# Two graph layers on one core: the edge features of a chunk loaded in two transfers of four tiles in place of one of eight

## The reference, cut

```python
def layer0(x, edge_attr_3, W, root, gamma, beta, src, dst):
    # B: [E, 8] products of the three attributes or their complements
    z = (B[:, :, None] * x[src][:, None, :]).reshape(E, 8 * 64)
    agg = segment_sum(z @ W.reshape(8 * 64, 64), dst)
    out = agg / max(cnt, 1)[:, None] + x @ root
    return elu(batchnorm(out, gamma, beta))

def layer1(x, edge_attr_64, W1, b1, W2, b2, gamma, beta, src, dst):
    agg = segment_sum(x[src] + edge_attr_64, dst)
    return batchnorm(relu(agg @ W1 + b1) @ W2 + b2, gamma, beta)

x = layernorm(x + layer0(x, ...))
x = layernorm(x + layer1(x, ...))
```

## Time and profile before

| | |
|---|---|
| median of 3 runs | 760.03 us |
| lowest, highest | 753.52, 762.93 us |
| profiled execution: span from first to last instruction | 739.4 us |
| profiled execution: whole time | not given; the median less the span is 20.6 us |
| TensorE, weight loads, VectorE busy | 575.8, 434.3, 448.4 us |
| ScalarE, GpSimd busy | 377.2, 382.3 us |
| DMA traffic | 48.70 MB, 89134 packets |

### The profile page before, as it was taken

The page is one execution under the profiler, slowest core; times in us unless marked ns, Lnnn a source line. Parts: engine busy times, 40 slices in busy tenths (PEclk is TensorE's granted clock), DMA queues, the critical chain, the costliest instruction groups (busy, mean ns, idle before and its releaser), DMA issues.

```text
span 739.4 us, 16650 instructions
## 1 busy us (share of the span) xinstructions
PE 575.8 (78%) x4151; PEld 434.3 (59%) x4152; DVE 448.4 (61%) x1622; ACT 377.2 (51%) x663; POOL 382.3 (52%) x382
## 2 busy tenths in 40 slices
PE   4455889688777878787877878877887679869994
PEld 2334667566665656676665656756666567734542
DVE  7934657455464646465564556645664567587975
ACT  8344656365555655565565566565632233343044
POOL 6873666466565656565566565666666662000000
PEclk9965888788997978899898989799997868779998
DMA  6421333233242323233233342442412150000002
GB/s 130 109 62 30 94 85 73 59 92 86 68 95 56 97 59 95 68 82 95 60 95 81 71 96 59 94 95 60 97 36 55 37 103 12 3 0 1 1 1 43
DMA packets 89134, 48.70 MB, mean 66 GB/s; under 512 B 76252, under 2 KB 77667, under 8 KB 89069
## 3 DMA queue, kind: packets, MB, share of 16 engines
q1 hardware_dynamic: 75949, 35.40, 19.8%
q0 software_dynamic: 11968, 12.28, 8.6%
q10 hardware_dynamic: 1152, 0.16, 0.2%
HBM read 46.86 MB, written 0.93 MB: 65 GB/s over the span
## 4 chain that ended last, share of the span: by engine, by line
PE 62%; issue 14%; DVE 9%; another core or an unknown queue 5%; DVEq 4%; ACT 2%; ACTq 0%
PE ps L678 14%; PE ps L601 13%; PE ps L638 13%; PE ps L623 5%; PE ps L861 5%; DVEq L1308 3%; PE ps L607 2%; PE ps L866 2%; PE ps L617 2%; DVE pair L1298 2%; DVE agg L1313 1%; PE ps L591 1%; PE ps L712 1%; PE ps L628 1%
## 5 line engine op out<-in xcount | busy, mean ns | idle before, releaser
L528 POOL DMA_INDIRECT rows<-in_x,idx x374 | 381.0, 1019 | 236.0 <-issue 94.1
L601 PE MATMUL ps<-pair,ohp 128*125 128x500 bf16 x416 | 186.0, 450 | 39.2 <-issue 14.4
L1002 ACT CAST adj<-ps 125x500 f32 x208 | 123.8, 595 | 180.6 <-remote 99.2
L678 PE MATMUL ps<-whot,rows 128*128 128x108 f32 x816 | 194.5, 323 | 17.1 <-issue 16.9
L638 PE MATMUL ps<-xs,u 125*128 125x192 bf16 x1050 | 155.3, 274 | 54.3 <-issue 46.2
L678 PEld LDWEIGHTS ps<-whot,rows 128*128 128x128 f32 x816 | 157.9, 229 | 34.9 <-issue 28.5
L1313 DVE TENSOR_TENSOR agg<-agg,ps 128x24 f32 x416 | 75.8, 182 | 151.8 <-remote 74.2
L989 ACT ACTIVATE u<-u,own 128x768 uint8<-128x768 uint8 (+1 forms) x168 | 152.7, 961 | 26.3 <-DMA u<-codes_scratch 25.9
L1298 DVE TENSOR_SCALAR pair<-iota_h,comb 128x500 bf16<-128x500 int16 x416 | 123.6, 358 | 61.8 <-remote 25.6
L638 PEld LDWEIGHTS ps<-xs,u 125*128 125x128 fp8e4 x1050 | 103.0, 111 | 96.2 <-issue 78.9
L1302 DVE TENSOR_SCALAR ohp<-iota_h,srcp 128x125 bf16<-128x125 int16 x416 | 109.8, 275 | 6.3 <-issue 5.1
(11 more groups left out here) (211 smaller groups left out, 383.4 us busy)
## 6 DMA issues: line engine op xcount, KB each, us to landing
u<-codes_scratch SPq DMA_DIRECT2D x42, 400.0 KB
rows<-in_edge_attr SPq DMA_DIRECT2D x51, 256.0 KB
rows<-in_x,idx POOLq DMA_INDIRECT x374
x_now<-in_x SPq DMA_DIRECT2D x25, 31.2 KB
adj<-in_x SPq DMA_DIRECT2D x1, 700.0 KB
xs<-in_x SPq DMA_DIRECT2D x1, 700.0 KB
out<-u SPq DMA_DIRECT2D x3, 224.0 KB
adj<-in_edge_attr SPq DMA_DIRECT2D x1, 576.0 KB
```

The source lines that it names most:

```text
L528: pool.indirect_dma_start(rows[:, s, t, 0:C], None, x, bass.IndirectOffsetOnAxis(ap=idx[:, at:at + 1], axis=0)).then_inc(gathered[0][0] if ...
L601: return nc.tensor.matmul(m_ps[0:PN, bank_of(phase, g), 0:PAIRS], ohp[:, par, t, :], pair[:, par, t, :], start=(n == 0), stop=(n == GROUP ...
L678: last = nc.tensor.matmul(z_ps[:, half, at:at + ZW], rows[:, s, t, :], whot[:, par, t, :], start=True, stop=True)
L1002: nc.scalar.copy(bass.AP(adj, offset=start, ap=[[NT * NA, PN], [NA, NT], [1, GWIN]]), m_ps[0:PN, bank_of(phase, g), 0:PAIRS].rearrange("p ...
```

## The change

Each load of the edge features becomes two, of tiles 0 to 3 and 4 to 7. The first waits for `z_done` of the first half of the slot's chunk, the second for that of the second half. Both count up the same semaphore, which so reaches 32 for a chunk, and TensorE waits for both at the chunk's first product. The last load (L479) becomes one of four tiles and one of three.

```diff
-            def load_ea(c, s):
-                sp.wait_ge(z_done, c * 2 + 2)
-                sp.dma_start(rows[:, s, :, C:P], ea64_full[:, bass.ds(c * CH, CH), :]).then_inc(ea_loaded[s], 16)
+            def load_ea(c, s, half):
+                sp.wait_ge(z_done, c * 2 + (half + 1))
+                at = half * (CH // 2)
+                sp.dma_start(rows[:, s, at:at + CH // 2, C:P], ea64_full[:, bass.ds(c * CH + at, CH // 2), :]
+                             ).then_inc(ea_loaded[s], 16)
...
             for s in range(SLOTS):
-                load_ea(s, s)
+                for half in range(2):
+                    load_ea(s, s, half)
...
             def load_chunk(i, s, taken_too=True):
                 c = i * SLOTS + s
-                load_ea(c, s)
+                for half in range(2):
+                    load_ea(c, s, half)
                 if s % STEP == 0:
                     load_x(i * (SLOTS // STEP) + (s // STEP - 1))
...
-            sp.dma_start(rows[:, SLOTS - 1, 0:CH - 1, C:P], ea64_full[:, FULL - CH + 1:FULL, :]).then_inc(
-                ea_loaded[SLOTS - 1], 16)
+            for half in range(2):
+                at, n = half * (CH // 2), CH // 2 - half
+                sp.dma_start(rows[:, SLOTS - 1, at:at + n, C:P],
+                             ea64_full[:, FULL - CH + 1 + at:FULL - CH + 1 + at + n, :]).then_inc(ea_loaded[SLOTS - 1], 16)
...
                     if t == 0:
-                        pe.wait_ge(ea_loaded[s], i * 16 + 16)
+                        pe.wait_ge(ea_loaded[s], i * 32 + 32)
...
-                pe.wait_ge(ea_loaded[s], i * 16 + 16)
+                pe.wait_ge(ea_loaded[s], i * 32 + 32)
```

## The result

The changed kernel takes 760.63 us (median of 20 runs, 754.79 to 766.0) against 761.75 us for the kernel before (20 runs, 753.52 to 770.64). The ratio of record is 1.0099, 95% interval [1.0064, 1.0135]: 1% slower, and no change at 2%. The two medians, 760.63 / 761.75 = 0.9985, say otherwise, and so do the means, 760.94 / 761.54 = 0.9992 with a half width of 0.0030 (from the scatter of both sets). The ratio of record leaves out runs that lie more than 1.5% above the fastest of their kernel, but that alone doesn't make the 1% here: it takes 3 of the 20 runs of the kernel before (765.1, 765.51 and 770.64 us), the mean of the other 17 is 760.56 us, and 760.94 / 760.56 = 1.0005. The reference that 1.0099 stands for, 760.94 / 1.0099 = 753.5 us, is as low as the lowest of the 20 runs. What the 1% is worth is thus the first question of the experiments.

A forecast was written before the change was run, and what follows sets the result against it. A chunk was taken as a ring of TensorE, VectorE and ScalarE with the codes beside it, the edge features off it. Terms summed to 0: 739.4 + 20.6 + 0 = 760 us, range 750 to 771.

The forecast's parts named there:

- the time around the span: Outside the profiled 739.4 us span: 20.6 us, taken from the 760.03 us median of three runs.
- (d): Start: four issues become eight, done by 24.2 us, under the codes issue at 24.58; term 0 to 0.1 us.
- (f): DMA engines: edge features issued behind the codes on SP's queue don't slow them; term 0, range -4 to +3 us.
- (a): First half's start: in 41 of 51 loads about 0.65 us behind the codes; nobody waits for it, term 0.
- (b): Second half's start: up to 0.65 us later, against 35 us of cover before TensorE needs it; term 0.
- The 27 us: Within (b): upper bound if the cover were gone, 41 x 0.65 us.
- (c): SyncE's own time: 52 more issues, 34 us, spread over a queue that stands waiting; term 0.
- The rival of 794 us: SyncE's queue: each of 52 further issues holds up the codes by 0.65 us, 34 us more; chance 1%.
- the 104 us: Added transfers: about 2 us fixed cost each, 52 x 2 us more if each were waited for.
- (e): End: last loads' halves start earlier; one more issue of 0.4 us lies in both covers; term 0.
- The slower rival (775 us): DMA engines: first half delays the codes by up to 0.67 us in 22 chunks, 15 us more; chance 6%.

The follow-up runs named there:

- three sets: Unedited changed kernel against the kernel before: the result 0.9992 and two repeats, 1.0012 and 1.0005 in the means; weighted together 1.0003 +- 0.0019.
- four transfers: Changed kernel with each chunk's load in four transfers of two tiles, against the kernel before: 759.13 against 758.31 us, means 1.0011, R 1.0040.
- with no cover: Edge loads issued three chunks later, just ahead of use, in the kernel before (whole) and changed one (split): 820.48 and 821.15 us, against 744.90 before.
- with the edge features away: Kernel before with its whole edge transfer issued half a chunk later, against the kernel before: 759.03 against 758.31 us, means 1.0010, R 0.9996.

## Why the prediction was right or wrong

**The forecast**, 760 us and no change, agrees with the two medians (760.63, 761.75) and with the pooled 1.0003 +- 0.0019. It doesn't agree with the ratio of record, whose interval leaves out 1: 1.0099 is some 7.5 us, where my sum had 0 and at most +3 us. If that ratio is right, the step that failed is that every term was put at 0, and which term holds the 7.5 us stays open. The runs don't show it in any: the means of three sets give 1.0003, four transfers cost no more than two, and the landing of the codes is 3.99 us as before. The kernel against itself gave 1.0037, so part of such a ratio is no kernel's; the rest of 1.0099 is unexplained. What the runs do show as wrong in the prediction are a step beside the terms (the time around the span), the size of (d) and the reading in (f).

**The sum around the span failed.** 739.4 + 20.6 was made from the span of one execution and a median that lies 2.5% from its time. What lies around the span is 2 us. That the number came out is no merit of the sum: I had taken the median as the anchor and then found the 20.6 us as the difference. A sum from durations alone would have given 741 us, which lies among the times of two of the chips and 2.5% under the result. The range, from the scatter of three runs, held for this set and the first chip of the experiments; on the other two the changed kernel or its relatives took 742 to 746 us in the mean.

**(a), when the first half starts:** right. 0.64 and 0.66 us behind the codes in the rows above, median 0.77. The change doesn't do what it says, as forecast, and the first half set ahead of the codes shows that doing it would have given nothing.

**(b), the second half:** right in the term, and the cover was more than enough: of the three chunks one is enough, and with none 76 us are lost. The 27 us that I allowed if the cover were gone were far too many: with no cover a split costs 0.7 us in the means (4 runs each), within their scatter (817.98 to 822.87 and 818.29 to 826.52). The step that failed there is that an issue moved by 0.65 us moves the landing by as much.

**(c), SyncE's time:** right; with four transfers it isn't felt either. The rival of 794 us is out, and so is the 104 us estimated from a fixed cost: with every transfer waited for, splitting them costs 0.7 us.

**(d), the start:** the term was right at the end of the account, its size was not. I bounded eight issues by 2 x 2.95 us, 0.74 us each, and held 24.2 us against 24.58; they took 8.50 us, 1.06 each, and the codes went at 27.98. One execution was too little for such a bound: four whole transfers took 2.95 to 4.23 us in five executions, eight halves 4.79 to 8.50 us in five. The cover that I named, the wait for `codes_stored`, was used up; another one that I hadn't named, VectorE's `xs` at 65 us, took it. That the term came out at 0 was luck in the argument, though not a narrow one: in four transfers a delay of 13.2 us was made good too.

**(e), the end:** right, 0.95 us for two issues, and the counts at 619.74, ahead of the last products at 656.0.

**(f), the DMA engines:** the step failed, the term held. "What is issued behind the codes on SP's queue doesn't slow them" was read from two landings; with the edge features away the median falls by 0.39 us. That these two landings agree with ring order wasn't enough: packets of the later transfer begin before the last of the earlier one has ended. This isn't a time in the span: ScalarE's wait for the codes is 25.9, 20.5 and 14.6 us in three kernels, and 18.0 us in the kernel before once more, with no trace of it in the run times. The slower rival (775 us) was right that the edge features delay the codes, and wrong in the size and the path. In the changed kernel the codes land after 3.99 us (median of 16), as before.

**The chances.** Same at 2% was 91%, and it was the case.

## What to carry to other kernels

A transfer that no engine waits for can be split, moved by half a chunk or by two chunks, and the time stays; look first for its name among the waits. An earlier wait condition does nothing where the queue that would see it stands at another wait in front. Before a term is set against one trace, ask from which chip the trace is: here the same kernel differs by 2% between chips and by as much between runs, so that a ratio of 1.01 was no finding until the kernel had been run against itself and the change repeated.

## What the runs showed of the hardware

- The same program took 758.3 us on one chip and 744.7 and 744.9 us on two others (means of 35, 35 and 23 runs). The granted clock was 0.837 in the mean of these runs on the first and 0.849 and 0.848 on the others. Within one chip, runs with 0.01 less of it took 2.5 to 3.0 us more (a line through its runs), so the clock makes an estimated 3 of the 13.5 us; the rest is open.
- What an issue from SyncE takes at the start varies between executions more than with the size of the transfer: four whole ones took 2.95 to 4.23 us (five executions, 0.74 to 1.06 us each), eight halves 4.79 to 8.50 us (five, 0.60 to 1.06), sixteen quarters 17.04 us (one, 1.07). In the loop a second half follows the first by 0.76 and 0.67 us in the rows above, and by 1.44 us in the kernel without cover.
- Two transfers issued one behind the other from SyncE overlap: of the edge features, issued a median 0.95 us behind the codes, about half of the packets began before the codes' last had ended (537 of 1024, median of 41 chunks of the kernel before, a few of them of x).
- A wait of 4.0 us on TensorE in every chunk costs 76 / 41 = 1.85 us a chunk. More than half of it was taken from other waits of the same ring of engines: TensorE's before the take fell from 78.9 us to 19.1 us.
